# Coupling stage of a fused adaLN, attention and FFN kernel: Tanh results into SBUF, one of VectorE's products on GpSimd, a sum moved to the last round, waits by half

## What is computed

```
def coupling_net(h):                       # 128 -> 128 -> 64 -> 32 -> 1
    h = gelu(h @ w1 + b1); h = gelu(h @ w2 + b2); h = gelu(h @ w3 + b3)
    return sigmoid(h @ w4 + b4)
def twist(x):
    o_r, o_i, p_r, p_i = split(x, 4)
    return concatenate([p_r, -p_i, -o_r, o_i])

for cycle in range(3):
    cp = factor from tanh(coupling_net) and a term per sequence   # cp = ar03 * tanh(.) + cB
    S, T = S + cp * T, T - cp * S
x = x + S
```

## Time and profile before

| | |
|---|---|
| median of 3 runs | 1015.61 us (1014.88 to 1015.79) |
| the profiled execution | 1016.32 us, span from first to last instruction 1015.0 us |
| granted TensorE clock, mean | 0.995 |
| busy, of the span | PE 96%, DVE 86%, ACT 82%, POOL 47% |

### The profile page before, as it was taken

How to read it: one execution, slowest core, us unless ns; L and a number is a source line. 1 busy time by engine, 2 the same in 40 slices (tenths; PEclk the granted TensorE clock), 3 DMA queues, 4 the chain that set the end, 5 groups by cost and what they waited for, 6 DMA issues and landing times.

```text
span 1015.0 us, 25983 instructions
## 1 busy us (share of the span) xinstructions
PE 978.4 (96%) x8953; PEld 790.3 (78%) x8953; DVE 874.3 (86%) x3714; ACT 831.8 (82%) x2232; POOL 476.7 (47%) x545
## 2 busy tenths in 40 slices
PE   8999999999999999999989999999999999999897
PEld 7898888889888889733268888888777777776566
DVE  6777989898989898799998999889978888896985
ACT  6988888888888888887797887876887888886786
POOL 4334545454545453607810111102888888893041
PEclk9999999999999999999999999999999999999899
DMA  9000000000000000000000000000000000000002
GB/s 376 34 2 2 2 2 2 2 2 2 2 2 2 2 2 2 1 1 1 0 1 1 1 1 1 4 9 11 23 23 23 23 24 22 23 3 1 1 2 84
DMA packets 8723, 18.31 MB, mean 18 GB/s; under 512 B 1296, under 2 KB 5648, under 8 KB 8208
## 3 DMA queue, kind: packets, MB, share of 16 engines
q1 hardware_dynamic: 8592, 16.65, 4.9%
HBM read 10.36 MB, written 2.10 MB: 12 GB/s over the span
## 4 chain that ended last, share of the span: by engine, by line
PE 78%; DVE 10%; ACT 6%; POOL 3%; issue 2%; DMA 0%; SPq 0%; DVEq 0%; ACTq 0%; POOLq 0%
PE PB L247 8%; PE PB L248 8%; PE PB L249 8%; PE PB L352 6%; PE PB L407 6%; PE PB L390 6%; PE PB L1822 5%; PE PB L1219 3%; PE PB L1794 3%; PE PB L1221 3%; PE PB L1220 3%; PE PB L1839 3%; PE PB L439 2%; PE PB L440 1%; PE PB L441 1%
## 5 line engine op out<-in xcount | busy, mean ns | idle before, releaser
L382 POOL TENSOR_TENSOR W<-W,small 128x512 f32<-128x512 f32 x128 | 138.6, 1083 | 210.6 <-DVE small L376 210.6
L371 ACT ACTIVATE W<-W,small 128x128 f32<-128x128 f32 x512 | 198.8, 391 | 29.6 <-DVE small L362 29.0
L247 PE MATMUL PB<-RR_s 128*128 128x256 f32 (+3 forms) x568 | 183.6, 323 | 3.7 <-DVE RR_s L265 2.2
L248 PE MATMUL PB<-RR_s 128*128 128x256 f32 (+3 forms) x568 | 176.1, 310 | 0.0
L249 PE MATMUL PB<-RR_s 128*128 128x256 f32 (+3 forms) x568 | 175.9, 310 | 0.0
L362 DVE CUSTOM_DVE_ANT_0 W<-PB,W 128x128 f32<-128x128 f32 x512 | 117.2, 284 | 39.0 <-PE PB L352 38.0
L1810 POOL TENSOR_TENSOR AR_s<-AR_s,small 128x512 f32<-128x512 f32 x128 | 129.5, 1042 | 15.5 <-DVE small L1803 15.4
L1193 ACT ACTIVATE AR_s<-PB,W 128x512 f32<-128x512 f32 (+2 forms) x160 | 100.6, 629 | 28.6 <-PE PB L249 22.8
L247 PEld LDWEIGHTS PB<-RR_s 128*128 128x128 f32 x568 | 107.7, 190 | 11.2 <-issue 4.3
L1207 DVE TENSOR_TENSOR RR_s<-AR_s,RR_s 128x512 fp32r<-128x512 f32 (+2 forms) x160 | 100.3, 636 | 17.5 <-ACT RR_s L1198 13.3
L1803 DVE CUSTOM_DVE_ANT_0 AR_s<-PB,W 128x128 f32<-128x128 f32 x512 | 111.0, 286 | 2.7 <-PE PB L1794 1.0
(11 more groups left out here) (388 smaller groups left out, 2448.5 us busy)
## 6 DMA issues: line engine op xcount, KB each, us to landing
W<-in_w SPq DMA_DIRECT2D x1, 5809.5 KB, 24.8
out<-XT SPq DMA_DIRECT2D x8, 256.0 KB, 2.3
W<-in_w SPq DMA_DIRECT2D x2, 512.0 KB, 5.5
W<-in_w SPq DMA_DIRECT2D x1, 1024.0 KB, 8.1
XF<-in_xT SPq DMA_DIRECT2D x1, 1024.0 KB, 11.3
W<-AR_s SPq DMA_DIRECT2D x16, 64.0 KB, 2.1
AR_s<-AR_s SPq DMA_DIRECT2D x16, 64.0 KB, 2.1
QS<-AR_s SPq DMA_DIRECT2D x12, 64.0 KB, 2.1
```

What stands on the lines that cost most here:

```text
L247: nc.tensor.matmul(out, lh, rh, start=True, stop=False)
L248: nc.tensor.matmul(out, ll, rh, start=False, stop=False)
L371: e = nc.scalar.activation(SS[r][:, hl], SS[r][:, hl], ACTF.Exp, bias=mx[r][:, h:h + 1], scale=-1.0, accum_out=rc[r][:, h:h + 1])
L382: nc.gpsimd.tensor_tensor(s3, s3, over(rc[r], 2, [128, 4, 128]), ALU.mult).then_inc(s_nrm, 1)
```

## The change

ACT's Tanh writes to SBUF: half 0 into `H2[p]`, half 1 into `H3[p]`, and the factors and the products cp * T are made in place there. The PSUM bank counts as free once the Tanh is done. For y < 2 VectorE does the halves in the order factor 1, factor 0, product cp * S of half 0, product cp * T and sum of half 0, then product cp * T and sum of half 1; the product cp * S of half 1 is now GpSimd's, ahead of its two subtractions. The sum of tokens and state is taken off the end of round 1 and put into GpSimd's queue at step 1 of round 2 (t = 12 to 15). ACT's wait for GpSimd is split by half and placed before the Gelu of that half, and its wait for VectorE's sums is at step 1. Two of the loads of tokens become one.

```diff
-        load_x(1024, 2048, s_x[1])
-        load_x(2048, 4096, s_x[2])
+        load_x(1024, 4096, s_x[1])
...
-            return (s_cs, 2 * m + s + 1) if m < 8 else (s_x2, 2 * (m - 8) + s + 1)
+            return s_tn, 2 * m + s + 1
...
         def act_g1(m, s):
+            if m >= 4:
+                act.wait_ge(s_ptw, 2 * (m - 4) + s + 1)
...
-            if y:
+            if y and st == 1:
                 act.wait_ge(s_cs, 2 * (m - 4) + 2)
-                act.wait_ge(s_ptw, 2 * (m - 4) + 2)
...
-                    nc.scalar.activation(bank3(("h4", m, s))[:, :], bank3(("h4", m, s))[:, :], ACTF.Tanh, bias=b4h2, scale=0.5).then_inc(s_tn, 1)
+                    nc.scalar.activation((H2, H3)[s][p], bank3(("h4", m, s))[:, :], ACTF.Tanh, bias=b4h2, scale=0.5).then_inc(s_tn, 1)
...
-            cps = [bank3(("h4", m, s))[:, :] for s in range(2)]
+            cps = [H2[p], H3[p]]
+            def factor(s): ...      # wait s_tn; cps[s] = cps[s] * ar03 + cB    -> s_cp
+            def turned(s): ...      # wait s_twc or s_ptw; cps[s] = cps[s] * T  -> s_cu
+            if y < 2:
+                factor(1)
+                factor(0)
+                dve.wait_ge(s_cp, 2 * m + 2)
+                nc.vector.tensor_tensor(cs(H1[p], 0), cps[0], cs(S, 0), ALU.mult).then_inc(s_ct, 1)
+                dve.wait_ge(s_ct, m + 1)
+                turned(0)
+                dve.wait_ge(s_cu, 2 * m + 1)
+                nc.vector.tensor_tensor(cs(S, 0), cps[0], cs(S, 0), ALU.add).then_inc(s_cs, 1)
+                dve.wait_ge(s_ctp, m + 1)
+                turned(1)
+                dve.wait_ge(s_cu, 2 * m + 2)
+                nc.vector.tensor_tensor(cs(S, 1), cps[1], cs(S, 1), ALU.add).then_inc(s_cs, 1)
+                return
...
         def pool_couple(p, y, st):
+            if y == 2 and st == 1:
+                for s in range(2):
+                    pool.wait_ge(s_cs, 2 * (m - 4) + s + 1)
+                    nc.gpsimd.tensor_tensor(cs(XF, 2 * p + s), cs(XF, 2 * p + s), cs(S, s), ALU.add).then_inc(s_pxs, 1)
...
+            pool.wait_ge(s_cp, 2 * m + 1)
+            nc.gpsimd.tensor_tensor(cs(H1[p], 1), H3[p], cs(S, 1), ALU.mult).then_inc(s_ctp, 1)
+            pool.wait_ge(s_ct, m + 1)
+            pool.wait_ge(s_cu, 2 * m + 1)
+            nc.gpsimd.tensor_tensor(cs(Tw, 0), cs(Tw, 0), cs(H1[p], 0), ALU.subtract).then_inc(s_ptw, 1)
+            pool.wait_ge(s_ctp, m + 1)
+            pool.wait_ge(s_cu, 2 * m + 2)
+            nc.gpsimd.tensor_tensor(cs(Tw, 1), cs(Tw, 1), cs(H1[p], 1), ALU.subtract).then_inc(s_ptw, 1)
```

More of the change, by code:

```diff
@@ L131, in build @@
         s_w = [signal(f"load_w{i}") for i in range(5)]
-        s_x = [signal(f"load_x{i}") for i in range(3)]
+        s_x = [signal(f"load_x{i}") for i in range(2)]
         s_xa = signal("load_xa")
@@ L296, in pool_xs @@
         def pool_xs(c):
-            pool.wait_ge(s_x[min(c // 4, 2)] if c else s_xa, 16)
+            pool.wait_ge(s_x[min(c // 4, 1)] if c else s_xa, 16)
             pool.wait_ge(s_set, 1)
@@ L832, in build @@
         s_cp, s_cu, s_ct, s_cs, s_x2 = signal("cpl"), signal("cpl_u"), signal("cpl_t"), signal("cpl_s"), signal("x2")
-        s_ptw, s_pxs, s_ag = signal("cpl_tw"), signal("x_plus_s"), signal("agg")
+        s_ptw, s_pxs, s_ag, s_ctp = signal("cpl_tw"), signal("x_plus_s"), signal("agg"), signal("cpl_t_pool")
         s_ad, s_adl, s_adm, s_hid = signal("adapt_dve"), signal("adapt_pool"), signal("adapt_mm"), signal("hidden")
@@ L1013, in dve_couple, with factor, turned @@
             dve.wait_ge(s_cxd, 1 if p < 3 else 4)
-            cps = [bank3(("h4", m, s))[:, :] for s in range(2)]
-            for s, cp in enumerate(cps if 0 in steps else ()):
+            cps = [H2[p], H3[p]]
+            def factor(s):
                 c = 2 * p + s
                 dve.wait_ge(s_tn, 2 * m + s + 1)
[L1018 to L1024, removed]
+                nc.vector.scalar_tensor_tensor(v4(cps[s]), v4(cps[s]), ar03, over(cB[:, 4 * c:4 * c + 4], 2, [128, 4, 128]), ALU.mult, ALU.add).then_inc(s_cp, 1)
+            def turned(s):
                 if y == 0:
@@ L1028, in dve_couple @@
                     dve.wait_ge(s_ptw, 2 * m + s - 8 + 1)
-                if y < 2:
-                    dve.wait_ge(s_ct, 2 * m + s + 1)
-                nc.vector.tensor_tensor(cp, cp, cs(Tw, s), ALU.mult).then_inc(s_cu, 1)
+                nc.vector.tensor_tensor(cps[s], cps[s], cs(Tw, s), ALU.mult).then_inc(s_cu, 1)
+            if y < 2:
[12 more added lines that the diff above has]
+                return
+            for s in range(2) if 0 in steps else ():
+                factor(s)
+            for s in range(2) if 2 in steps else ():
+                dve.wait_ge(s_cp, 2 * m + s + 1)
+                turned(s)
             for s, cp in enumerate(cps if 3 in steps else ()):
@@ L1034, in dve_couple @@
                 dve.wait_ge(s_cu, 2 * m + s + 1)
[L1035 to L1039, removed]
+                dve.wait_ge(s_pxs, c + 1)
+                nc.vector.tensor_tensor(cs(XF, c), cp, cs(XF, c), ALU.add).then_inc(s_x2, 1)
         def pool_couple(p, y, st):
```

## The result

The changed kernel takes 1054.19 us (median of 4 runs, 1052.17 to 1054.57) beside 1015.70 for the kernel before on the same chip: a ratio of 1.0379, interval 1.0367 to 1.0391. It is slower by 38.5 us. The profiled execution took 1054.57 us with a span of 1053.3, 38.3 more than before's 1015.0.

A forecast was written before the change was run, and what follows sets the result against it. VectorE was taken to bound the coupling stage. Terms 23.7 + 11.7 + 0.9 + 5.2 + 1.1 - 1.3 = 41.3 us, less 1.3, gave +40 and a forecast of 1056 us, range 1036 to 1068.

The forecast's parts named there:

- The bound: Coupling stage: VectorE sets the pace at 4.90 us per update, with PE a close second.
- Exclusion: VectorE instructions with two SBUF inputs and GpSimd's take whole turns, 1.08 us per GpSimd instruction, 0.90 for L1116; chance 0.72.
- No gain from SBUF by itself: VectorE's update instructions get no faster from SBUF operands alone: 0.61 us pitch, like those from PSUM.
- The update: Each y < 2 update takes 8.85 us against 4.90, +3.95; at t = 12 and 13, 10.75, +5.85 each.
- Round 2: Four token sums and the last L1116 cost 5.2 us on the first update; two L1171 add about 1.1.
- Split waits, load, banks: ACT's split waits before the Gelus give back 1.3 us; the larger token load and earlier PSUM banks give 0.
- VectorE's new wait: VectorE waits for GpSimd's product before its own last product; done two places earlier, so the wait costs nothing.
- No exclusion: Rival: VectorE's SBUF instructions run beside GpSimd as PSUM ones do; 1016 us, give or take 2; chance 0.07.
- faster: Rival: no exclusion, dependent neighbours cost nothing and GpSimd catches up at t = 9; 1012 us; chance 0.05.
- Exclusion at half price: Rival: VectorE keeps the path while its queue is full, GpSimd works in its stalls; +20, 1036 us; chance 0.08.
- A slower PE: Rival: idling PE's clock falls to 1.2 GHz, matmuls take over 9 us per update; about +8, 1064; chance 0.08.
- the 1.3: Taken off the 41.3 us sum because GpSimd's product may be shorter and some token sums may fall into VectorE's reductions.

The follow-up runs named there:

- e1: Kernel before with only Tanh and the updates moved to SBUF, the PSUM bank free after the Tanh; 1048.26 us, ratio 1.0325.
- e2: Changed kernel with Tanh back in PSUM and both products on VectorE; new order, split waits, moved sums and single load kept; 1018.98 us, ratio 1.0033.
- e4: Changed kernel with half 0's Tanh in PSUM and only half 1's in SBUF; 1032.71 us, ratio 1.0175.
- e7: Separate probe without the reference: twelve VectorE and six GpSimd 128x512 instructions, alone and together; twelve with SBUF inputs took 7.31 us alone, 13.71 together.
- e6: Kernel before with ACT's waits split by half and the token sums moved to step 1 of round 2; 1013.84 us, ratio 0.9984.
- e5: Kernel before with only the two loads of tokens made one; 1015.04 us, ratio 1.0001.
- e8: Separate probe without the reference: 40 repetitions shifting when GpSimd's pair meets VectorE's twelve SBUF instructions; no GpSimd instruction over 1.84 us.

## Why the prediction was right

**The bound.** VectorE set the pace before and does so after: 1.2 us of idle time in the stage, PE and ACT waiting for it.

**Exclusion, the step on which it all hung.** It came as predicted. e1 shows that operands in SBUF are the cause in this kernel, e2 that without them (and without GpSimd's product) 3.8 of the 32 us remain in the updates, e4 that half the operands give about half the loss, and e7 the price by itself, 1.07 us. The Trainium skill (SBUF — State Buffer, section "Who interferes with whom") calls the shared port pair an exclusive lock between VectorE and GpSimd; the trace agrees, by the ends 1.13 and 0.55 us apart.

**No gain from SBUF by itself.** Twelve products at 7.31 us from two SBUF inputs and 7.26 with one of them in PSUM confirm that the operands' place is worth nothing alone. The other rule weighed ahead of the result, of 58 and 120 cycles of fixed cost (the Trainium skill, VectorE: DVE Perf Modes, the section on the TRN2 errata), is not what the probe shows: by it the PSUM form would be the slower one.

**The update.** 8.85 predicted, 8.70 measured in the fourth and sixth; with two token sums 10.75 predicted, 10.60 and 10.58 measured; the one with the left-over L1116 9.75 and 9.47. The four turns of GpSimd fall where they were laid: a split between the two factors, the product ahead of VectorE's, a subtraction after either sum. The 0.15 lies in the two factors. I had them at 0.66 + 1.08 = 1.74 and 0.66 + 0.90 = 1.56; by their ends they take 1.67 (509.08 to 510.75) and 1.50 (to 512.25), so a turn costs VectorE the same from end to end beside a factor as beside a product.

**Where the sum was off.** For the eight updates I had 23.7 + 11.7 + 0.9 - 1.3 = 35.0, measured +32.0. The second and third rose by 2.2 and 2.9, 1.7 and 1.1 us less than the 3.95 predicted. The second has no split of weights in it, and its last subtraction meets a small instruction (L610, 1.13 us) that had waited for GpSimd in the kernel before too (L611 there, 0.85); so the third has one turn fewer. The prediction had left this small work out of its collisions. The first took 11.07, 0.6 more than 6.47 + 3.95. There the split missing from the second falls on small work (L1106, 1.08 us, where it was 0.28), and VectorE is held under two instructions of GpSimd in a row:

```profile
456.74 3.23 DVE L1032 TENSOR_TENSOR AR_s<-HR,HF 128x512 f32<-128x512 f32 x1
...
457.12 1.08 POOL L1131 TENSOR_TENSOR RR_s<-W,RR_s 128x512 fp32r<-128x512 f32 x1
458.16 1.25 POOL L1063 TENSOR_TENSOR AR_s<-HR,HF 128x512 f32<-128x512 f32 x1
```

**Round 2.** Predicted +5.2 for the four token sums and the L1116, and 1.1 for L1171; measured +5.2 in all, and +5.9 on the first group, where it was predicted to fall:

```profile
530.17 3.25 DVE L1019 SCALAR_TENSOR_TENSOR HR<-HR,small 128x512 f32<-128x512 f32 x2
533.35 3.42 DVE L1026 TENSOR_TENSOR HR<-HR,XT 128x512 f32<-128x512 f32 x2
536.69 3.42 DVE L1051 TENSOR_TENSOR XF<-HR,XF 128x512 f32<-128x512 f32 x2
...
554.26 5.16 POOL L1186 TENSOR_TENSOR RR_s<-XF,RR_s 128x512 fp32r<-128x512 f32 x1 [6.32 <-ACT RR_s L1175]
```

The first group takes 11.29 us where it took 5.44. The table counts from first factor to first factor, so the last subtraction of the eighth update, which I had laid in that update, stands under round 2: six turns, 6.1 us, and not five. The first L1171 (L1186 here) cost 0.5, and 0.7 of waits that the kernel before has in round 2 are gone. That the two 5.2 agree is thus in part chance. The second L1171 cost VectorE nothing, where it had cost 0.55 before: in the last row it is GpSimd that is held, for 5.16 us, under VectorE's instructions, which keep their pitch.

**Split waits, load, banks.** e6 gives 1.6 us for the waits and the sums (0.7 to 2.6; in its profile 1.1 in the updates and 0.8 in round 2), 1.3 predicted (its two smaller waits are 0.21 and 0.25, so 1.10 and both of them would have made 1.6); e5 nothing for the load; VectorE's new wait is hidden in the changed kernel, as predicted, and e4 shows what it costs once that cover is gone.

**The start.** The stage begins 1.8 us later in the profiled execution than in that of the kernel before, which I hadn't foreseen. From 9 to 13 us PE's granted clock is 0.57 there (row above) and 1.00 in the kernel before, which would take 4.0 x 0.43 = 1.7 us of work at full clock from PE (an estimate). That this is what made the start late is not shown: in e5 the stage begins at 454.3, 0.8 later than before, at a clock of 1.00. e2 to e5, which all have the larger load, begin it between 452.9 and 454.3, so the load by itself isn't the cause; what lowered the clock in that execution stays open.

**The rivals.** No exclusion (1016) and faster (1012) fell with e1 and e7. Exclusion at half price (1036) fell with the update of 8.70: GpSimd's instructions don't wait for VectorE's pauses as a rule. A slower PE: the clock did fall to 1.2 GHz in parts of the stage, as that rival said, but PE's matmuls still fitted under VectorE, 4.69 of 5 us between 530 and 535; the 8 us did not come.

**What is luck in the total.** The sum was 41.3, and 40 after 1.3 were taken off. The reason for the 1.3 did not come true: the product took 1.25 us where nothing held it, so it isn't of a shorter kind, and the eight token sums took 1.71 on average, none of them in a reduction. The stage cost 32.0 + 5.2 = 37.2, 4.1 less than the sum. The late start, 1.8 us that nobody had predicted, makes up part of it: without it the execution would be 36.5 us slower and not 38.3. The mechanism and the price of a turn are right; that the total came within 2 us of 1056 is in part chance.

## What to carry to other kernels

Before an operand of VectorE moves from PSUM to SBUF, look at what GpSimd does at that time: here each 128x512 instruction of GpSimd that read SBUF and met such VectorE work cost about 1.08 us, while beside VectorE work with an input in PSUM it cost nothing. Work given to GpSimd relieves VectorE only where that holds; in the changed kernel taking three instructions per update back to VectorE made it about 10 us faster, some 2 of which were the start. Read both engines' timelines side by side by the ends of instructions, since busy time counts a held instruction as work.

## What the runs showed that I had not expected

Who is let in first is not settled by a simple turn. In the probes the two engines alternate in all 40 repetitions, with 1.84 us as the longest GpSimd instruction, yet in the full kernels GpSimd is held for 6.1 us (e1, at 469) and 5.16 us (changed kernel, at 554), and VectorE for 3.23 us (at 456). In the first two, VectorE instructions that started after GpSimd's had been issued went ahead of it, seven and six of them, so the prediction's sentence that whichever issues first keeps the other out doesn't order these cases. In the kernel before, e2 and e6, with an operand in PSUM, no such instruction of GpSimd in the stage takes over 1.3 us. The cause wasn't found; a stretch of offsets is untried, as said under e8.

A VectorE instruction that depends on the one just before starts 0.73 us after it rather than 0.60, with operands in PSUM too: five such places make e2's update 5.56 us instead of 4.90, and an order that puts an independent instruction between them is free.

It isn't only the forms with two SBUF inputs that are held: tensor_scalar, whose one input lies in SBUF, took 10.53 us for twelve beside six of GpSimd (8.26), while the product with one input in SBUF and one in PSUM stayed at 7.26. The probe has no group of twelve tensor_scalar alone; in the kernel before, one of this size with GpSimd idle reads

```profile
444.97 0.42 DVE L526 TENSOR_SCALAR AR_s<-AR_s 128x512 f32<-128x512 f32 x1
```

and the next instruction starts at 445.31, 0.34 later. By an estimate from that, twelve alone take 4.2 us, and the rest is (10.53 - 4.2) / 6 = 1.06 us for each instruction of GpSimd, the same price. TENSOR_REDUCE was not held and held nothing: in the changed kernel L1186, started at 546.66 beside three of VectorE's reductions, took 1.28 us, and the three (0.79 us together) kept their pitch. And GpSimd's fills, which read nothing, disturb nothing: the twelve SBUF products of VectorE took 7.31 us beside six fills (2.85 us).
